# The key bias of a linear-attention kernel: added by DVE on the way out of the bank, instead of by a product on PE

## The reference, cut to what matters

```python
q = _split_heads(x @ Wq + bq)
k = _split_heads(x @ Wk + bk)
v = _split_heads(x @ Wv + bv)
q = jax.nn.elu(q) + 1.0
k = jax.nn.elu(k) + 1.0
k = k / jnp.sqrt(jnp.sum(k * k, axis=-1, keepdims=True) + EPS)
scores = jnp.einsum('bhqd,bhkd->bhqk', q, k)
attn = jnp.einsum('bhqk,bhkd->bhqd', scores, v)
...
out = attn @ Wo + bo          # then x + out, layer norm; x + that, layer norm
...
h = jax.nn.silu(fp4_linear(x, w_gate)) * fp4_linear(x, w_up)
return fp4_linear(h, w_down)  # then x + that, layer norm
```

## Time and profile before

| | |
|---|---|
| median of 3 runs | 791.17 us (791.04 to 791.76) |
| the profiled execution | 793.14 us, span 791.4 us |
| busy in the span | PE 749.1 us (95%), DVE 584.1 (74%), POOL 602.2 (76%), ACT 479.4 (61%) |
| first phase, steps 0 to 31 | from PE's first projection at 18.9 us to about 242 us |
| second phase's first own step | DVE L801 at 247.1 us, after the reload of x_plus |
| bias products (L336) | 64, from 18.9 to 236.9 us, 380 ns each in the median |

### The profile page before, as it was taken

The page is one execution under the profiler, slowest core; times in us unless marked ns, Lnnn a source line. Parts: engine busy times, 40 slices in busy tenths (PEclk is TensorE's granted clock), DMA queues, the critical chain, the costliest instruction groups (busy, mean ns, idle before and its releaser), DMA issues.

```text
span 791.4 us, 13643 instructions
## 1 busy us (share of the span) xinstructions
PE 749.1 (95%) x4162; PEld 631.6 (80%) x4162; DVE 584.1 (74%) x1432; ACT 479.4 (61%) x878; POOL 602.2 (76%) x891
## 2 busy tenths in 40 slices
PE   1999999999997599999999999999999999999996
PEld 1767777777775388888888888988888888888886
DVE  2578875555544578888888888888888888888765
ACT  2465665555553466767666676767676666666654
POOL 2488886676666889887878787878878787878766
PEclk9999999999999599999999999999999999999999
DMA  8133233333322210111111111111111111200001
GB/s 272 50 121 117 84 121 120 120 121 120 108 92 87 74 54 27 45 64 49 46 41 67 41 54 41 63 45 54 41 44 65 47 48 41 67 14 28 14 28 41
DMA packets 22188, 54.95 MB, mean 69 GB/s; under 512 B 2530, under 2 KB 5476, under 8 KB 22116
## 3 DMA queue, kind: packets, MB, share of 16 engines
q1 hardware_dynamic: 20992, 53.29, 19.5%
q10 hardware_dynamic: 1124, 0.79, 0.4%
HBM read 28.90 MB, written 25.17 MB: 68 GB/s over the span
## 4 chain that ended last, share of the span: by engine, by line
PE 79%; DVE 8%; POOL 4%; issue 4%; ACT 3%; DMA 2%; ACTq 0%; POOLq 0%; DVEq 0%; SPq 0%
PE banks L314 23%; PE banks L315 19%; PE banks L316 19%; PE banks L435 7%; PE banks L412 6%; PE banks L350 2%; PE banks L336 2%; DMA gamma_b<-in_L_attn_gamma_dram 1%; PE banks L325 1%; DVE lnbuf L651 1%; DVE arena L688 1%; DVE arena L701 1%; DVE arena L694 1%; ACT arena L512 1%; ACT arena L515 1%
## 5 line engine op out<-in xcount | busy, mean ns | idle before, releaser
L314 PE MATMUL banks<-wgu_hi,actT_lo 128*128 128x512 f32 (+1 forms) x384 | 155.8, 406 | 1.7 <-DVE actT_lo L778 1.7
L315 PE MATMUL banks<-wgu_lo,actT_hi 128*128 128x512 f32 (+1 forms) x384 | 143.8, 375 | 0.0
L316 PE MATMUL banks<-wgu_hi,actT_hi 128*128 128x512 f32 (+1 forms) x384 | 143.6, 374 | 0.0
L584 ACT ACTIVATE arena<-banks 128x512 f32<-128x512 f32 x64 | 38.2, 597 | 146.5 <-PE banks L316 146.5
L314 PE MATMUL banks<-wd_hi,actT_lo 128*128 128x256 f32 (+1 forms) x384 | 124.9, 325 | 0.0
L974 POOL TENSOR_TENSOR arena<-arena 128x960 f32<-128x960 f16 (+2 forms) x68 | 117.6, 1729 | 0.0
L954 POOL TENSOR_TENSOR arena<-arena 128x704 f32<-128x704 f32 x64 | 89.2, 1393 | 33.2 <-DVE arena L765 33.2
L315 PE MATMUL banks<-wd_lo,actT_hi 128*128 128x256 f32 (+1 forms) x384 | 108.1, 282 | 0.0
L316 PE MATMUL banks<-wd_hi,actT_hi 128*128 128x256 f32 (+1 forms) x384 | 107.8, 281 | 0.0
L778 DVE TENSOR_TENSOR actT_lo<-banks,actT_hi 128x512 fp32r<-128x512 f32 (+1 forms) x132 | 83.2, 669 | 16.0 <-ACT actT_hi L578 15.8
L963 POOL TENSOR_TENSOR lnbuf<-lnbuf,gamma_b 128x256 f32<-128x256 f32 x64 | 46.9, 733 | 53.9 <-ACT lnbuf L591 53.4
(11 more groups left out here) (113 smaller groups left out, 1867.7 us busy)
## 6 DMA issues: line engine op xcount, KB each, us to landing
x_plus_scratch<-xs SPq DMA_DIRECT2D x32, 512.0 KB, 2.9
xs<-x_plus_scratch SPq DMA_DIRECT2D x32, 512.0 KB, 3.2
arena<-in_L_attn_x_dram SPq DMA_DIRECT2D x32, 256.0 KB, 3.5
out_dram<-arena SPq DMA_DIRECT2D x32, 256.0 KB, 2.1
resid<-in_L_ffn_w_down_dram SPq DMA_DIRECT2D x1, 704.0 KB, 8.9
resid<-in_L_ffn_w_gate_dram SPq DMA_DIRECT2D x1, 640.0 KB, 8.8
resid<-in_L_ffn_w_up_dram SPq DMA_DIRECT2D x1, 640.0 KB, 10.5
resid<-in_L_attn_Wk_dram SPq DMA_DIRECT2D x1, 256.0 KB, 4.8
```

The source lines that it names most:

```text
L314: nc.tensor.matmul(dst, sl, mh, start=(k == 0 and not begun), stop=False, skip_group_check=shared)
L315: nc.tensor.matmul(dst, sh, ml, start=False, stop=False, skip_group_check=shared)
L316: last = nc.tensor.matmul(dst, sh, mh, start=False, stop=(k == n - 1), skip_group_check=shared)
L584: nc.scalar.activation(gact[:, 0:G0], ps[:, G_BANK, :], ACT.Silu).then_inc(g_act, 1)
```

## The change

The rows product goes, with the rows and what made them. bk is loaded broadcast to all 128 partitions, and DVE adds 1 to it once (`bk_one`). In each step DVE has a new first instruction on the keys, `k_bias`: it reads the keys' half of the two banks, adds bk_one and writes the copy kb (128 by 512) in SBUF. ACT's exp and DVE's maximum read kb. On DVE, v_bias now stands ahead of k_features. PE may overwrite the banks once k_bias (not k_features) of two steps before is done.

```diff
-            def split_product(dst, stat, mov, n, begun=False, shared=False):
+            def split_product(dst, stat, mov, n):
...
             def kv_project(p):
                 pe.wait_ge(xT_lo_s, p + 1)
-                after(pe, k_feat, p - 1)
+                after(pe, k_lin, p - 1)
                 after(pe, v_s, p - 1)
...
-                    nc.tensor.matmul(ps[:, bank, 0:D], rows[:, D:], rows[:, 0:D], start=True, stop=False,
-                                     skip_group_check=True)
...
-            act.dma_start(rows_st[:, 0:D], bk.partition_broadcast(2)).then_inc(rows_in, 16)
+            act.dma_start(bk_one[:, :], bk.partition_broadcast(P)).then_inc(rows_in, 16)
...
             def k_exps(p):
-                act.wait_ge(kv_ps, p + 1)
+                act.wait_ge(k_lin, p + 1)
                 after(act, k_feat, p)
-                b = kv_banks(p)
-                nc.scalar.activation(kexp, ps[:, b:b + 2, 0:D], ACT.Exp, bias=mone[:, :]).then_inc(k_exp, 1)
+                nc.scalar.activation(kexp, kb, ACT.Exp, bias=mone[:, :]).then_inc(k_exp, 1)
...
-                    act.wait_ge(rows_st_s, 1)
-                    nc.scalar.activation(rows_hi[:, :], rows_st, ACT.Copy).then_inc(rows_hi_s, 1)
...
             def k_features(p):
                 dve.wait_ge(k_exp, p + 1)
                 after(dve, k_hat, p - 1)
+                nc.vector.scalar_tensor_tensor(out=kf[:, p % 2, :].rearrange("p (j c) -> p j c", j=2), in0=kexp, scalar=1.0,
+                                               in1=kb, op0=ALU.min, op1=ALU.max).then_inc(k_feat, 1)
+
+            def k_bias(p):
+                dve.wait_ge(kv_ps, p + 1)
+                after(dve, k_feat, p)
+                after(dve, k_exp, p)
                 b = kv_banks(p)
-                nc.vector.scalar_tensor_tensor(out=kf[:, p % 2, :].rearrange("p (j c) -> p j c", j=2), in0=kexp, scalar=1.0,
-                                               in1=ps[:, b:b + 2, 0:D], op0=ALU.min, op1=ALU.max).then_inc(k_feat, 1)
+                nc.vector.tensor_tensor(kb, ps[:, b:b + 2, 0:D], bk_one[:, :].unsqueeze(1).broadcast_to([P, 2, D]),
+                                        ALU.add).then_inc(k_lin, 1)
...
-                    dve.wait_ge(rows_hi_s, 1)
-                    nc.vector.tensor_tensor(rows[:, 0:D], rows_st[:, 0:D], f32(rows_hi[:, 0:D]),
-                                            ALU.subtract).then_inc(rows_lo_s, 1)
-                    nc.vector.tensor_copy(rows[:, D:], f32(rows_hi[:, D:])).then_inc(rows_s, 1)
-                    dve.wait_ge(rows_lo_s, 1)
-                    nc.vector.tensor_copy(rows[0:1, 0:D], f32(rows_hi[0:1, 0:D])).then_inc(rows_s, 1)
...
                 if pair(p):
+                    k_bias(p)
+                    v_bias(p)
                     k_features(p)
-                    v_bias(p)
...
-            nc.vector.tensor_scalar(rows_st[:, 0:D], rows_st[:, 0:D], 1.0, None, ALU.add).then_inc(rows_st_s, 1)
+            nc.vector.tensor_scalar(bk_one[:, :], bk_one[:, :], 1.0, None, ALU.add).then_inc(bk_one_s, 1)
```

More of the change, by code:

```diff
@@ L73, in build @@
         headmask = sb("headmask", [P, P])
-        rows_hi = sb("rows_hi", [2, D + P], F32R)
-        rows = sb("rows", [2, D + P], F32R)
-        gamma_b, beta_b, bo_b, bv_b = (sb(n, [P, D]) for n in ("gamma_b", "beta_b", "bo_b", "bv_b"))
+        gamma_b, beta_b, bo_b, bv_b, bk_one = (sb(n, [P, D]) for n in ("gamma_b", "beta_b", "bo_b", "bv_b", "bk_one"))
         bq_c, bq_neg, bq_one = (sb(n, [P, KT]) for n in ("bq_c", "bq_neg", "bq_one"))
@@ L103, in build @@
         vb = take(3 * 2 * D).rearrange("p (r j c) -> p r j c", r=3, j=2)
+        kb = take(2 * D).rearrange("p (j c) -> p j c", j=2)
         kexp = take(2 * D).rearrange("p (j c) -> p j c", j=2)
@@ L138, in build @@
         wam, wsn, ws14, winv = (lnbuf[:, i * NB:(i + 1) * NB] for i in range(4))
-        rows_st = lnbuf[0:2, 4 * NB:4 * NB + D + P]
         def halves(y):
@@ L171, in build @@
         watt_hi, watt_lo = sem("watt_hi"), sem("watt_lo")
-        rows_st_s, rows_hi_s, rows_lo_s, rows_s = sem("rows_whole"), sem("rows_hi"), sem("rows_lo"), sem("rows_done")
+        bk_one_s, k_lin = sem("bk_plus_one"), sem("k_linear")
         w_amax, w_nudged, w_scale_s, w_scaled, w_f16, w_half, w_rounded, w_deq = (
@@ L309, in _ @@
         def _(pe):
-            def split_product(dst, stat, mov, n, begun=False, shared=False):
+            def split_product(dst, stat, mov, n):
                 for k in range(n):
                     (sh, sl), (mh, ml) = stat(k), mov(k)
-                    nc.tensor.matmul(dst, sl, mh, start=(k == 0 and not begun), stop=False, skip_group_check=shared)
-                    nc.tensor.matmul(dst, sh, ml, start=False, stop=False, skip_group_check=shared)
-                    last = nc.tensor.matmul(dst, sh, mh, start=False, stop=(k == n - 1), skip_group_check=shared)
+                    nc.tensor.matmul(dst, sl, mh, start=(k == 0), stop=False)
+                    nc.tensor.matmul(dst, sh, ml, start=False, stop=False)
+                    last = nc.tensor.matmul(dst, sh, mh, start=False, stop=(k == n - 1))
                 return last
@@ L335, in kv_project @@
                     c = slice((p % PPB) * 2 * P + jj * P, (p % PPB) * 2 * P + (jj + 1) * P)
-                    nc.tensor.matmul(ps[:, bank, 0:D], rows[:, D:], rows[:, 0:D], start=True, stop=False,
-                                     skip_group_check=True)
                     last = split_product(ps[:, bank, :], lambda k: (xT_hi[:, k, c], xT_lo[:, k, c]),
-                                         lambda k: (wkv_hi[:, k, :], wkv_lo[:, k, :]), KT, begun=True, shared=True)
+                                         lambda k: (wkv_hi[:, k, :], wkv_lo[:, k, :]), KT)
                 last.then_inc(kv_ps, 1)
@@ L388, in first @@
                     pe.wait_ge(watt_lo, 1)
-                    pe.wait_ge(rows_s, 2)
                 if pair(p):
@@ L408, in attend @@
                 if u == 0:
-                    pe.wait_ge(k_feat, MERGE)
+                    pe.wait_ge(k_lin, MERGE)
                     pe.wait_ge(v_s, MERGE)
@@ L544, in first @@
                     act.wait_ge(cols_set, 2)
-                    act.wait_ge(small_set, 4)
+                    act.wait_ge(small_set, 3)
                 if p >= 7 and (p - 7) % PPB == 0:
@@ L637, in _ @@
             nc.vector.memset(eps_k[:, :], EPS_K).then_inc(small_set, 1)
-            nc.vector.memset(rows_st[:, D:], 1.0).then_inc(small_set, 1)
             nc.vector.memset(eps_v[:, :], EPS_LN).then_inc(mv_set, 1)
@@ L723, in first @@
                     dve.wait_ge(consts_set, 4)
+                    dve.wait_ge(bk_one_s, 1)
                 if p >= 6 and (p - 6) % PPB == 0:
```

1 line of the change is left out of this document (removed).

## The result

| | before | after |
|---|---|---|
| median | 791.31 us (790.70 to 792.89, 11 runs) | 793.48 us (792.77 to 794.95, 11 runs) |
| ratio, 95% interval | | 1.0025 (1.0016 to 1.0034) |
| profiled execution, span | 793.14, 791.4 us | 793.02, 791.3 us |
| granted clock, mean | 0.984 | 0.975 |

The change makes the kernel 0.25% slower, about 2 us. So each kernel was traced a second time (`again` and `after_again` in the experiments), and what follows rests on all four traces.

The account below looks back on a forecast made before the run. Limits named: a loop through POOL in the first phase's steps 0 to 13, PE in steps 14 to 31. Terms -1.6+2.5+5.5-6.2+0.55 = +0.8 us gave 792.0 on the median basis; range 783.5 to 799, narrower 789 to 796.

Parts of the forecast that it names:

- k_features against POOL: With two SBUF inputs, k_features waits out POOL's first bias addition, ending at t+4.44 (t: seed exp); loop 6.08+0.21 = 6.29 us.
- rival A: k_features doesn't wait for POOL: stage two's loop is 6.08 us, POOL isn't delayed, 783.3 us in all; chance 0.14.
- POOL's loss: POOL's second bias addition waits for k_features, 0.55 us a step; steps 4 to 13 grow by 5.5 us.
- Rival B: k_features waits, but POOL loses little behind it: steps 4 to 13 only +2.0 us, total 787.9; chance 0.17.
- C: POOL's second addition goes ahead of waiting k_features: loop 7.54 us, +26 us in all, some 817; chance 0.05.
- Steps 1 to 3: Early first-phase steps: k_features pushes small DVE instructions behind a later POOL one, plus POOL's delay in step 3: +2.5 us.
- Stage two: Steps 14 to 30: 17 loops of 6.29 us plus small extras, 108.6 against 114.83 us: -6.2 us.
- Changeover: Before the second phase: k_features pushes POOL's last addition, whose rows the reload waits for, once more: +0.55 us.
- rival E: PE's granted clock at the changeover may shift between levels: 2 us either way in every case; no chance of its own.
- Start: Before step 1: DVE work gone -0.7, larger bk load +0.3, two bias products gone at PE's slower rate -1.2: -1.6 us.
- v_bias costs nothing in front: v_bias ahead of k_features on DVE fits, with k_bias, in the 1.39 us k_features waits for the exp: no cost.
- D: The loop is 0.2 to 0.5 us longer than summed, through later PE products or POOL waits: 795 to 800; chance 0.19.

Follow-up runs that it names:

- again: The kernel before, unchanged, traced and timed a second time: 792.11 us against 792.21, ratio 0.9999.
- after_again: The changed kernel, unchanged, traced and timed a second time: 794.10 us against 792.40 for the kernel before, ratio 1.0025.
- bank: vlate with k_bias's sum written back into the bank, exp and maximum reading it there, PE waiting for k_features: 790.46 us, 0.9977 of the kernel before.
- vlate: The changed kernel with v_bias moved behind k_features on DVE: 801.59 us, 1.0116 of the kernel before.
- peorder: The changed kernel with q_project ahead of kv_accumulate on PE: 792.31 us, 0.9996 of the kernel before.
- early_bank: early with the sum written back into the bank, v_bias ahead of k_bias, PE waiting for k_features: 775.28 us, 0.9783 of the kernel before.
- early: The changed kernel with k_bias and v_bias ahead of q_features on DVE, the sum still in SBUF: 781.71 us, 0.9851 of the kernel before.

## Why the prediction was right, and where it wasn't

792.0 was forecast and 793.48 measured, inside the narrower range too, and on the side (over by 0.25%) that I had given 0.41. As a difference it is less good: +0.8 was the sum, +2.2 is measured. The mechanism is the forecast's. Its terms:

**k_features against POOL: right to 0.02 us.** It was to end 0.02 plus 512/960 us behind the first bias addition of POOL (L918, L911 after), which is 0.55, and does: 0.55 in step 4 and in this step of stage two.

```profile
151.69 0.21 ACT L501 ACTIVATE arena<-arena 128x32 f32<-128x32 f32 x1
...
153.17 0.75 DVE L669 SCALAR_TENSOR_TENSOR resid<-banks,bq_one,arena 128x512 f32<-128x512 f32 x1 [1.03 <-ACT arena L510]
153.84 0.68 DVE L686 TENSOR_TENSOR arena<-banks,bk_one 128x512 f32<-128x512 f32 x1
...
154.30 1.28 POOL L911 TENSOR_TENSOR xs<-arena,bo_b 128x512 f32<-128x512 f32 x1
154.55 0.72 ACT L515 ACTIVATE arena<-arena,mone 128x512 f32<-128x512 f32 x1 [1.41 <-DVE arena L686]
155.31 0.82 DVE L678 SCALAR_TENSOR_TENSOR arena<-arena 128x512 f32<-128x512 f32 x1 [0.19 <-ACT arena L515]
155.53 1.75 POOL L911 TENSOR_TENSOR xs<-arena,beta_b 128x512 f32<-128x512 f32 x1
```

L678 ends at 156.13, t+4.44 as forecast. Its median is 0.82 (0.8 to 0.95 forecast). So rival A (783.3), no wait at all, falls. Its price may have been near: bank has no wait and takes 790.46 with v_bias behind k_features, and less the 7 us between vlate and after that would be 783, an estimate. The rule of the Trainium skill (SBUF — State Buffer, "Who interferes with whom") agrees, for a scalar_tensor_tensor too: 0.82 with two SBUF inputs, 0.69 with one in a bank.

**POOL's loss: right in kind, 0.45 and not 0.55.** The second L911 takes 1.73 in the mean of steps 4 to 13 where it took 1.28; 0.45 a step against my 0.55, for POOL's instruction ends 1.15 us behind k_features (156.13 to 157.28) and not the full 1.28. Steps 4 to 13 grow by 4.9 instead of 5.5. Ten times 0.45 is 4.5 of it, if each step takes over what POOL loses; that is an estimate. No run takes the hold away and leaves k_bias and v_bias where after has them, and bank, which has no hold and v_bias behind, grows by 4.2 there through DVE's own list. Rival B (787.9) had this loss at nothing. C (POOL's second addition gets in ahead of the waiting k_features, 817) didn't come in any step of after.

**Steps 1 to 3:** +1.65 for +2.5; a guess between 0.8 and 3, and no run takes it apart.

**Stage two: -4.7 for -6.2, the largest miss.** The loop was to be 6.29 and is 6.31 to 6.32 in eleven of 17 steps; two with ACT's copy of the output products are 6.38 and 6.39, half of my +0.14. Steps 14 and 15 (7.29, 6.60) are 1.3 over the loop, forecast 1.0, and step 30 (6.52) is 0.2 over. What I hadn't seen is one step of 7.46, at 177.01 (waits of stage two, then PE, DVE and ACT in the timeline):

```profile
PE banks L346 <- DVE arena L705: 7.0, 4, 2.3
```

```profile
177.05 0.41 DVE L705 TENSOR_TENSOR arena<-banks,headmask 128x256 f32<-128x256 f32 x1
...
177.61 1.13 PE L346 MATMUL banks<-arena 128*128 128x128 f32 x8 [2.33 <-DVE arena L705]
...
178.81 0.62 PE L313 MATMUL banks<-actT_lo,wq_hi 128*128 128x512 f32 x1
179.23 0.63 PE L314 MATMUL banks<-actT_hi,wq_hi 128*128 128x512 f32 x1
...
182.44 0.60 PE L323 MATMUL banks<-ident,arena 128*128 128x128 f32 x4
```

```profile
183.08 0.60 ACT L483 ACTIVATE actT_hi<-banks 128x512 fp32r<-128x512 f32 x1 [0.96 <-PE banks L323]
...
184.05 0.32 ACT L498 ACTIVATE arena<-arena,eps_k 128x32 f32<-128x32 f32 x1
```

PE waits 2.33 us for mask_heads, which stands on DVE behind the sums and x_low; then its products come 0.42 apart instead of 0.23, and the granted clock is 0.83 in the stretch from 176 to 186 (1.00 in the ones before and behind). So the next transposes of x (L323) come late, ACT's copy of them (L483) waits 0.96 us for them, and the seeds (L498), which stand behind it in ACT's order, are late with it. That one step costs 1.15 us. peorder, which has the projection done before that wait, has no such step and is 1.3 shorter in stage two, with the clock low there as well; so it takes the late projection at the lower clock, and not the clock alone. Step 30 has a wait of 2.32 us and slow products in the same place. My sum had the loop and no term for a PE that idles: an engine that stops being the bound gets gaps, and its clock can go with them.

**Changeover:** +0.8 for +0.55. Step 31 has 0.18 of it (6.13 before, 6.31 after), and what follows it +0.56 and +0.69 in the two traces of after, which fits the +0.55 for POOL's last addition. Step 31 was missing from the sum. The granted clock of the earlier trace rows (0.57) is 0.53 in after, 0.77 in again and 0.90 in after_again: rival E is a scatter between executions of one kernel, not an effect of the change.

**Start: -1.6 forecast, about -0.5 in the medians.** DVE's low part of the key and value weights (L722, L714 after) was to end at 18.17 and ends at 18.25:

```profile
15.90 1.26 POOL L911 TENSOR_TENSOR xs<-arena,beta_b 128x512 f32<-128x512 f32 x1
...
16.48 1.77 DVE L714 TENSOR_TENSOR wkv_lo<-resid,wkv_hi 128x1024 fp32r<-128x1024 f32 x1
```

It is held until L911's end and gains 0.6 where 0.7 was forecast. The -1.2 for two bias products at PE's slower rate is not shown: the moment at which PE goes from 0.43 to 0.23 between products moves by more than that between traces (last section).

**v_bias costs nothing in front:** right: DVE is still idle for 0.19 us between it and k_features (row at 155.31). Behind k_features it costs 7 us (vlate).

**D** (loop longer by 0.2 to 0.5): the loop is only 0.02 longer. The sum of what is shown, -0.5 + 1.65 + 4.9 - 4.7 + 0.8, is +2.15; the first term was taken from the medians (2.17 apart), so this is no check of the sum. Against the forecast the terms miss by +1.1, -0.85, -0.6, +1.5 and +0.25. The answer was right by the mechanism, and that it is within 1.5 us is partly luck: misses of both signs cancel.

## What to carry to other kernels

An operation moved off the bounding engine is paid in the chain that comes second: write that chain down hand-over by hand-over, and put the new instruction where its engine waits anyway. Here the same bias addition makes a kernel of 775 us (early_bank) or of 802 (vlate), by its place and by where its sum lies. On DVE, look where each input lies: in these runs, beside a POOL that adds SBUF tiles, the maximum of a bank and a tile takes 0.69 us always, and the maximum of two tiles waits (0.82 to 1.70) and makes POOL wait (1.73 for 1.28). And a difference of 0.3% isn't in two traces; compare stage by stage over two traces of each kernel.

## What I had not expected of the hardware

**DVE and POOL take turns in the order of issue.** In after (step 4), k_features is issued in the last 0.28 us of POOL's first addition and 0.24 ahead of the second: it waits out the first, and the second waits for it. In `early` it is issued 0.1 us behind the second, and waits that out, as the rows of early above show: 1.70 us. So, by these two rows, being issued 0.34 us later on DVE turns a wait of 0.14 into one of 1.0. Rival C priced a longer wait still (2.15 us for k_features); its condition (POOL overtaking a k_features already issued) is met in no step. The price is regular: in every step of after where k_features waits 0.13 us or more, it ends 0.55 behind the POOL instruction that runs, and the POOL addition issued behind it ends 1.12 to 1.16 behind k_features. In step 1 it goes the other way round: k_features is issued 0.1 ahead of POOL's normalising product, takes its 0.69, and the product takes 1.51 for 1.06.

**The moment at which PE speeds up in the first pair** lies 3.1 to 7.3 us behind its first 512-column product in the twelve traces, where that product starts between 18.23 and 19.40: 7.3 and 6.8 in the two of before, 3.6 and 3.9 in the two of after, but 6.1, 6.4 and 6.4 in vlate, early and peorder, whose PE does the same in its first pair as in after. Before (products 0.43 apart until then), PE in the timeline:

```profile
26.37 0.50 PE L314 MATMUL banks<-wkv_hi,actT_lo 128*128 128x512 f32 x1
26.71 0.40 PE L315 MATMUL banks<-wkv_lo,actT_hi 128*128 128x512 f32 x1
```

and after:

```profile
18.30 0.79 PE L312 MATMUL banks<-wkv_hi,actT_lo 128*128 128x512 f32 x1 [0.51 <-DVE wkv_lo L714]
...
21.85 0.40 PE L314 MATMUL banks<-wkv_hi,actT_hi 128*128 128x512 f32 x1
22.08 0.39 PE L312 MATMUL banks<-wkv_hi,actT_lo 128*128 128x512 f32 x1
```

The first seed exp moves with it: 27.18 and 27.32 in after and after_again, 28.55, 28.07 and 28.69 in vlate, early and peorder. So one trace can't tell what a change at the start is worth to better than 1.5 us.
